# The turn from attention to feed-forward in a transformer layer on 8 cores: one of Z's buffers moved, GpSimd's and ScalarE's steps put in another order, loads issued at other places, and one tile's x1 written first in bf16

## The reference, cut to what matters

```python
x = x0 + attn(layernorm(x0))
x = x + ffn(layernorm(x))

def attn(src):                      # linear attention, post-norm block
    Q, K = elu(src @ Wq + bq) + 1, elu(src @ Wk + bk) + 1
    v = src @ Wv + bv
    KV = einsum('bshd,bshm->bhdm', K, v)               # sum over all 4096 tokens
    Z = 1 / (einsum('bshd,bhd->bsh', Q, K.sum(1)) + EPS)
    o = einsum('bshd,bhdm,bsh->bshm', Q, KV, Z)
    x = layer_norm(src + o @ Wo + bo, g1, be1)         # "x1" below
    y = gelu(x @ W1 + b1) @ W2 + b2                    # 1024 -> 4096 -> 1024
    return layer_norm(x + y, g2, be2)

def ffn(x):                         # Wf below: weight.T with disha added in
    return x @ weight.T + pooled(x) @ disha            # pooled: 16 groups of 64 channels summed
```

## Time and profile before

| | us |
|---|---|
| median of 3 runs | 1567.32 |
| lowest run | 1565.68 |
| profiled execution, its own time | 1555.34 |
| its span, by core | 1546.1 to 1553.4 |
| TensorE busy (page, core 1) | 1497.2 (96%) |
| VectorE busy | 977.3 (63%) |
| ScalarE busy | 516.4 (33%) |
| GpSimd busy | 418.4 (27%) |

### The profile page before, as it was taken

One profiled execution on the slowest core, in us unless ns is written; L12 is line 12 of the kernel. 1 busy time (PEld: TensorE's weight loads), 2 busy tenths in 40 slices (PEclk: granted clock), 3 DMA queues, 4 the chain that ended last, 5 costly groups with the idle time before them and its releaser, 6 DMA issues.

```text
span 1552.0 us, 26610 instructions; the slowest of 8 cores (1546.1 to 1553.4 us)
## 1 busy us (share of the span) xinstructions
PE 1497.2 (96%) x9240; PEld 889.7 (57%) x9240; DVE 977.3 (63%) x1082; ACT 516.4 (33%) x923; POOL 418.4 (27%) x404
## 2 busy tenths in 40 slices
PE   5999999998779999999999999999999999999997
PEld 2444444444446666666666666666666666666664
DVE  4676666658448575666767585665667585766234
ACT  2444444445413223232323323232323233232221
POOL 3323233222365222222231222222231222222111
PEclk9999999999899999999999999999999999999999
DMA  9979988877941312121221223121221213121121
GB/s 202 210 178 183 211 184 204 178 193 156 175 117 69 90 53 77 49 87 49 76 76 60 80 53 89 48 75 55 82 76 48 89 54 90 48 76 55 55 69 41
DMA packets 141024, 157.52 MB, mean 101 GB/s; under 512 B 94688, under 2 KB 102880, under 8 KB 140896
## 3 DMA queue, kind: packets, MB, share of 16 engines
q1 hardware_dynamic: 119568, 123.06, 26.8%
q0 software_dynamic: 14112, 25.70, 12.3%
q10 hardware_dynamic: 7216, 7.08, 1.4%
HBM read 117.53 MB, written 41.94 MB: 103 GB/s over the span
## 4 chain that ended last, share of the span: by engine, by line
PE 88%; DMA 5%; DVE 3%; issue 2%; POOL 2%; ACT 1%; SPq 0%; DVEq 0%; ACTq 0%; POOLq 0%
PE psH L1379 27%; PE psY L1357 26%; PE psY L611 12%; PE psS L892 7%; PE psS L710 6%; PE psS L582 6%; DMA arena<-Wv 2%; DMA arena<-WfT 2%; DMA qt_s<-arena 1%; DVE arena L820 1%; PE psH L590 1%; PE psS L797 1%; POOL arena L1217 0%; PE psY L582 0%; POOL arena L356 0%
## 5 line engine op out<-in xcount | busy, mean ns | idle before, releaser
L1379 PE MATMUL psH<-arena 128*128 128x256 bf16 x4096 | 533.1, 273 | 0.0
L1357 PE MATMUL psY<-arena 128*128 128x512 bf16 x2000 | 518.2, 381 | 8.0 <-ACT arena L1279 7.6
L1279 ACT ACTIVATE arena<-psH,arena 128x256 bf16<-128x256 f32 x512 | 242.9, 475 | 759.0 <-PE psH L1379 757.2
L1379 PEld LDWEIGHTS psH<-arena 128*128 128x128 bf16 x4096 | 402.0, 98 | 143.3 <-issue 0.3
L1357 PEld LDWEIGHTS psY<-arena 128*128 128x128 bf16 x2000 | 196.2, 98 | 137.6 <-issue 11.7
L820 DVE RECIPROCAL arena<-arena 128x512 f32<-128x512 f32 x60 | 200.8, 3346 | 72.1 <-ACT arena L810 72.1
L611 PE MATMUL psY<-arena 128*128 128x512 bf16 x944 | 213.2, 379 | 0.7 <-DVE arena L512 0.7
L611 PEld LDWEIGHTS psY<-arena 128*128 128x128 bf16 x944 | 91.0, 98 | 105.2 <-issue 1.1
L759 POOL TENSOR_TENSOR arena<-arena 128x1024 f32<-128x1024 f32 x32 | 68.8, 2154 | 230.4 <-ACT arena L755 222.3
L705 POOL TENSOR_TENSOR arena<-arena 128x1024 f32<-128x1024 f32 x32 | 68.1, 2128 | 229.8 <-ACT arena L700 229.8
L333 POOL TENSOR_TENSOR arena<-arena 128x1024 f32<-128x1024 f32 x29 | 67.7, 2333 | 201.8 <-DVE arena L518 201.3
(11 more groups left out here) (129 smaller groups left out, 1304.4 us busy)
## 6 DMA issues: line engine op xcount, KB each, us to landing
arena<-x SPq DMA_DIRECT2D x64, 512.0 KB, 4.8
xb_s<-arena SPq DMA_DIRECT2D x32, 512.0 KB, 6.0
arena<-W POOLq DMA_DIRECT2D x64, 256.0 KB, 7.9
arena<-xb_s SPq DMA_DIRECT2D x32, 512.0 KB, 3.2
out<-arena SPq DMA_DIRECT2D x31, 512.0 KB, 2.9
arena<-qt_s SPq DMA_DIRECT2D x16, 512.0 KB, 3.2
qt_s<-arena ACTq DMA_DIRECT2D x26, 256.0 KB, 8.4
arena<-WfT SPq DMA_DIRECT2D x16, 256.0 KB, 2.8
```

Source lines behind the costliest of these rows:

```text
L1279: sc.activation(h_buf(n)[:, :], hbank[n % 2], AF.Gelu, bias=b1c[:, c:c + 1]).then_inc(b_g, 1)
L1357: ii = te.matmul(ybank[k], h_buf(n)[:, (k // 2) * P:(k // 2 + 1) * P], w2_v[c][:, (k % 2) * HALF:(k % 2 + 1) * HALF], start=(c == 0), stop ...
L1379: ii = te.matmul(hbank[n % 2], w1_v[c // NCH][:, w, (c % NCH) * P:(c % NCH + 1) * P], x1T[i % 2][:, w, :], start=(w == 0), stop=(w == NCH ...
```

## The change

1. `ring(1, even)` moves to a free place, so `den_out(1, 0)` no longer waits for the q stores; `den_out(1, 1)` does.
2. GpSimd: four of the last five W2 loads are issued before W1 part 1. Part 2 is issued before the factors of pair 0 (`t_rstd(0, ..)`) instead of behind them. Part 3 waits for the q stores. The factors of pair 1 move up by two sums of Wf each.
3. SyncE: the first two pieces of Wf are loaded before the last q stores.
4. Tile 1 (`0, 1`): VectorE writes x1 straight into `nb` in bf16, and once more in float32 behind it; ScalarE's `x1_cast(0, 1)` is gone. TensorE does `q_proj(62)` before the transposes.
5. `last_prep` moves before the last tile's K addition, and `src_norm(0, ..)` before its exp. ScalarE inverts Z's last part before `q_exp(57)`, and VectorE scales with it before `m_out(15)`.
6. gelu 0 waits for all but the last q chunk, gelu 2 for all; `src_norm` moves to other steps; `b2_add` waits for the float32 x1 too.

```diff
@@ ring, pool_a, act_a, dve_a
         def ring(j, k):
             if j == 1:
-                return VF(W + 40960 + 2048 * (k % 2), HALF)
+                return VF(W + (55296, 40960)[k % 2], HALF)
...
+            w2_load(27)
+            w2_load(28)
...
+                if t == T - 1:
+                    sc.wait_ge(f_nm, 1)
+                    src_norm(sc, 0, 0)
+                    src_norm(sc, 0, 1)
                 k_exp(t)
...
-                if t == T - 1:
-                    last_prep(v)
                 k_in(t)
                 k_out(t)
                 if t < T - 1:
                     q_out(v, 2 * (t - 4))
+                if t == T - 2:
+                    last_prep(v)
@@ b2_add, den_out
             gp.wait_ge(b_x1b, 2 * j + sub + 1)
+            gp.wait_ge(b_x1, 2 * j + sub + 1)
...
-            elif j == 1:
+            elif j == 1 and k == 1:
                 sc.wait_ge(s_qst[1], 32 * NG)
@@ wf_in, sync_f
+        def wf_in(sy, h):
+            c, lo = h // 2, HALF * (h % 2)
+            sy.dma_start(zring[h % 2], wf_d[c * P:(c + 1) * P, lo:lo + HALF]
+                         ).then_inc(s_wf[h % 2], 16)
...
-            sy.wait_ge(b_src, 2)
             x_in(sy, 1, 0)
             x_in(sy, 1, 1)
             sy.dma_start(qs1[:, :, :, :], qt_d[1]).then_inc(s_q1, 16)
             q_store(sy, NG - 2, 1)
+            sy.wait_ge(f_q, 4)
+            for h in range(2):
+                wf_in(sy, h)
             q_store(sy, NG - 1, 0)
             q_store(sy, NG - 1, 1)
@@ pool_f
             bo_add(gp, 0, 1)
+            for c in (29, 30):
+                gp.dma_start(w2_v[c][:, :], w2_d[c * P:(c + 1) * P, :]).then_inc(s_w2, 16)
...
-            t_rstd(gp, 0, 0)
-            t_rstd(gp, 0, 1)
             gp.wait_ge(f_m, 16)
             for w in range(NCH):
                 gp.dma_start(w1_v[2][:, w, :],
                              w1_d[w * P:(w + 1) * P, 2 * D:3 * D]).then_inc(s_w1[2], 16)
+            t_rstd(gp, 0, 0)
+            t_rstd(gp, 0, 1)
             gp.wait_ge(a_q, NCH * NG)
+            gp.wait_ge(s_qst[1], 32 * NG)
             for w in range(NCH):
                 gp.dma_start(w1_v[3][:, w, :],
...
-            for c in range(27, NFCH):
-                gp.dma_start(w2_v[c][:, :], w2_d[c * P:(c + 1) * P, :]).then_inc(s_w2b, 16)
+            c = NFCH - 1
+            gp.dma_start(w2_v[c][:, :], w2_d[c * P:(c + 1) * P, :]).then_inc(s_w2b, 16)
@@ act_f, dve_f
             m_out(12)
+            z_inv(3)
             q_exp(sc, QL + 3)
-            z_inv(3)
...
-            x1_cast(sc, 0, 1)
...
             m_out(14)
+            z_mul(3)
             m_out(15)
             q_out(v, QL + 3)
-            z_mul(3)
...
             t_stats(v, 0, 1)
+
+            hm, n = home(0, 1), 2
+            v.wait_ge(b_mvt, n)
+            v.scalar_tensor_tensor(hm[:, :], hm[:, :], mvt[1][:, 0:1], g1b[:, :], ALU.subtract,
+                                   ALU.mult).then_inc(b_gt, 1)
             q_out(v, QL + 5)
-            x1(v, 0, 1)
-            for n in range(QL + 6, NCH * NG):
+            v.wait_ge(b_gt, n)
+            v.wait_ge(b_rt, n)
+            v.wait_ge(b_tx, 1)
+            v.scalar_tensor_tensor(nb[:, :], hm[:, :], rt[1][:, 0:1], be1b[:, :], ALU.mult,
+                                   ALU.add).then_inc(b_x1b, 1)
+            q_out(v, QL + 6)
+            v.scalar_tensor_tensor(hm[:, :], hm[:, :], rt[1][:, 0:1], be1b[:, :], ALU.mult,
+                                   ALU.add).then_inc(b_x1, 1)
+            for n in range(QL + 7, NCH * NG):
                 q_out(v, n)
@@ pe_f, sync_b
             q_proj(te, QL + 7)
+            q_proj(te, QL + 8)
             x1_tr(te, 0, 1, hbf)
-            q_proj(te, QL + 8)
             q_proj(te, QL + 9)
...
-                sy.wait_ge(f_q, 4)
-                for h in range(16):
...
+                for h in range(2, 16):
+                    sy.wait_ge(b_ws, h - 1)
+                    wf_in(sy, h)
@@ pool_b, act_b
-                for h in range(4, 10):
+                for h in range(4, 8):
                     w_sum(h)
                 t_rstd(gp, 1, 0)
-                w_sum(10)
-                w_sum(11)
+                w_sum(8)
+                w_sum(9)
                 t_rstd(gp, 1, 1)
-                for h in range(12, 16):
+                for h in range(10, 16):
                     w_sum(h)
...
                 if n == 0:
+                    sc.wait_ge(a_qt, NCH * NG - 1)
+                    sc.wait_ge(s_rows, 48)
+                elif n == 2:
                     sc.wait_ge(a_qt, NCH * NG)
-                    sc.wait_ge(s_rows, 48)
...
-                if c in (5, 7) and not post:
-                    src_norm(sc, 1, (c - 5) // 2)
+                if c in (2, 5) and not post:
+                    src_norm(sc, 1, c // 4)
...
-                if c == 28 and far:
+                if c == (28 if post else 30) and far:
                     src_norm(sc, i + 2, 0)
@@ y_step
             if n == 0:
-                te.wait_ge(s_w2, 16 * 27)
+                te.wait_ge(s_w2, 16 * (NFCH - 1))
...
-            if n == 27:
-                te.wait_ge(s_w2b, 16 * (NFCH - 27))
+            if n == NFCH - 1:
+                te.wait_ge(s_w2b, 16)
```

More of the change, by code:

```diff
@@ L986, in z_inv @@
                 sc.activation(zring[k % 2], zring[k % 2], AF.Exp, scale=-1.0).then_inc(f_z, 1)
-            sc.wait_ge(f_nm, 1)
-            src_norm(sc, 0, 0)
-            src_norm(sc, 0, 1)
             q_exp(sc, QL)
@@ L1175, in sync_b @@
                 sy.dma_start(dsh2[:, :], dsh_d).then_inc(s_dsh, 16)
-                sy.wait_ge(f_q, 4)
-                for h in range(16):
-                    c, lo = h // 2, HALF * (h % 2)
-                    if h >= 2:
-                        sy.wait_ge(b_ws, h - 1)
-                    sy.dma_start(zring[h % 2], wf_d[c * P:(c + 1) * P, lo:lo + HALF]
-                                 ).then_inc(s_wf[h % 2], 16)
+                for h in range(2, 16):
+                    sy.wait_ge(b_ws, h - 1)
+                    wf_in(sy, h)
                 sy.wait_ge(b_ws, 16)
```

## The result

The changed kernel took 1555.22 us in the median (1551.18 to 1557.54, five runs), the kernel before 1566.95 (1564.39 to 1721.02, five runs): ratio 0.9927, 95% interval 0.9903 to 0.9952. That is 11.7 us gained where 22.3 were forecast, and the time is 0.2 us outside the range. The profiled execution took 1551.18 us.

What follows compares the result with a forecast made beforehand. TensorE's 27 us of idle time and 7.1 us of clock between 345 and 490 us gave a 34 us ceiling; shifts summed to 16.1 at `attn(1, 0)`, then 21.2, then 22; 1567.3 - 22.3 = 1545 us, range 1538 to 1555.

Steps and rivals of the forecast that it cites:

- What costs nothing: Side effects held free: early W2 loads, and eight part 2 issues (4.6 us) before tile 0's factor, with 3 us of cover.
- The second rival: GpSimd is held issuing part 2 until part 1 lands; tile 0's factor 8 us late, gain 17 to 18, 1549 us; 17%.
- End of the passes: Last tile's K addition: with `last_prep` a tile earlier, TensorE's wait at the column sums goes; 1.1 us.
- Z's last part: Block 0: ScalarE no longer does `q_exp(57)` before inverting Z's last part, so TensorE gets the result 1.1 us earlier.
- Tile 1: Transposes of tile 1: `q_proj(62)` fills the wait and the cast leaves the chain; 2.9 of 3.6 us won.
- gelu: Gelu's table load no longer waits for the last `q_out`: 0.9 of 2.7 us won, bounds 0 and all of it.
- Z of pair 1: `den_out(1, 0)` no longer waits for the q stores: 4.9 us won; 1.1 us more from VectorE's wait before `attn(1, 0)`.
- T: The landing of the last q stores, taken as 403.5 us, with bounds 398.1 (quiet) and 409.7 (as slow as before).
- as slow as before: Upper bound of the q stores' landing: T = 409.7; everything behind D moves by 6 us, gain 16, 1551 us; 12%.
- The transpose at the twentieth step: Pair 1's factor runs before two sums of Wf, saving 5 us; 3.1 of TensorE's 8.1 us wait stay.
- D: Landing of the last casting load, from which GpSimd's fourth sum of Wf starts: 440.5 us before, forecast 424.4.
- Clock: TensorE's mean clock of 0.94 costs 7.1 us; 4.1 come back by `attn(1, 0)`, about 1 us more later.

Runs made afterwards that it cites:

- the factors first: Changed kernel with GpSimd's factors of pair 0 ahead of the eight loads of W1 part 2 again: 1539.39 us, ratio 0.9792.
- the split version: Changed kernel with five loads of W1 part 2 ahead of pair 0's factors, three behind: 1537.60 us, ratio 0.9777; run again 1537.79 us, ratio 0.9743.
- the two versions with more semaphores: Changed kernel, no instruction moved, W1 part 1's loads on eight semaphores instead of one: 1536.35 us, ratio 0.9829; on two: 1537.69 us, one execution.
- the half ring: Changed kernel with GpSimd's descriptor ring halved (`dynamic_dma_scratch_size` 1024 for 2048): 1567.17 us, one execution.

## Why the prediction was wrong

**The step that failed** is the one in "What costs nothing": "Eight issues of 0.57 us now precede the factor of tile 0 ... done by 376 ... That is 3 us of cover." 0.57 us is right for each issue (0.53 measured), but the eight are not one stretch: the fifteenth unfinished load is the sixth of part 2, and it waits until part 1 has landed. On core 0 the factor ran 36.5 us after the first product of the column sums, where the step had it due at 379.3 - 355.3 = 24.0; without the hold it ran at 23.8 to 26.3. Price: 8 to 9 us to the end.

**The second rival is what happened**, with 17%, and it was mis-sized three ways. It named part 2's fourth load as the fifteenth, by counting the two early W2 loads; both had landed (5.3 to 6.0 us after issue) and the hold came two loads later. It let part 1 land at 384.5, 29.2 us after the column sums' first product; it was 33.1 to 34.6. Part 1 was issued 0.8 us later than that working has it, and its slowest load took 23.6 to 25.0 us, for 20.4 in the earlier trace rows (20.3 to 21.8 over the cores). The two W2 loads are not shown to be the reason, since part 1's first load took as long as before (9.7 to 11.2 us for 9.9 to 11.2), nor is part 2, since with the factors first it was issued after part 1 had landed and the slowest load still took 23.2 to 24.6. Two pieces of Wf are now loaded in that time; that was not tested. And it let the loss shrink to 4 or 5 us at the twentieth step, since the sums of Wf were to be late anyway; but with the hold TensorE's own way is the later one there, no wait is left at those transposes on any core, and the whole 8 to 9 stay.

**Without the hold the sum was right, in part by luck.** In the split version attention (2, 0) starts 112.1 us after the first product of the column sums, 21.1 earlier than before in the median of the cores. The forecast of 22.3 was made on core 1, whose own mark before is 134.4, so it says 112.1 as well. On the way there it was off: attention (1, 0) was to start at 418.5 - 355.3 = 63.2 and started at 66.6, and the transposes of (1, 0) at 85.5 and started at 86.8. Most of the 3.4 us of delay went into the wait that the forecast had left at those transposes, and the rest was made good behind them: from there to attention (2, 0) it is 25.3 us for 28.0 before. By terms:
- *End of the passes, 1.1, and Z's last part, 1.1*: no wait at L1124's successor, and the transposes of tile 0 at 29.5 to 29.6 on the three cores without a wait for the first q load, for 31.9: both terms are there. On the other cores that wait, of up to 2.3 us, takes them away again (30.8 in the median). "What costs nothing" had put it at nothing; before there was none.
- *Tile 1, 2.9, and gelu, 0.9*: taken back, 3.7 and 0.7 us.
- *Z of pair 1, 4.9 and 1.1*: taken back, 3.2 to 4.1. T was forecast 48.2 us after the first product; the last store landed at 50.5 to 53.6, nearer to the bound "as slow as before" (54.4), so ScalarE still waits up to 4.5 us for `den_out(1, 1)` and TensorE up to 2.5. The term is 2 too large; the rest of the 3.4 us lies in the clock's share and in the wait for the q load, which no run separates.
- *The transpose at the twentieth step, 5.0 and a wait of 3.1 left*: taken back, 5.2 to 6.6; 0.6 to 0.8 of wait left in the median, up to 3.3. D as the start of the sums was not borne out: the fourth sum started at 68.3 to 74.4 (the forecast has 69.4), and on every core 3.0 to 4.5 us before the last casting load had landed.
- *Clock*: 0.94 became 0.96 in the changed kernel and 0.99 in the split version (core 4):

```profile
345.00:490.00 145.00, 134.04 (x852) 80.15 (x867) 104.89 (x112) 61.50 (x105) 69.78 (x71) 0.99 0.65 147
```

Of the 21 us some 18 to 19 reach the mean span. The 21.1 us are whole at every attention of the later blocks (the last starts 1077.8 us after the first product before, 1056.7 in the split version), so the rest is lost at the end: from TensorE's last product to the end of the span it is 4.3 to 5.4 us on the eight cores of the split version, and 3.4 to 3.6 on seven of before's. Why stays open.

**The rule of the Trainium skill** on GpSimd's descriptors beside a busy VectorE ("SBUF — State Buffer", section "SBUF: two separate sides") was rightly left out of the sum: the issues took 0.53 to 0.63 us with VectorE busy, before and after, and the long idle time follows the landings in every version. These runs do not test the rule itself: it is about operations that take both ports, and beside part 1 VectorE mostly ran casts out of PSUM (0.7 us each). Its 1557 us, 2 from the result, would have been right by accident. The Trainium skill's rule that queues are served packet by packet ("DMA: Bandwidth & Descriptors", section "Queues, rings and completion order") doesn't make a store quick here: under load they took 9.6 to 14.1 us on core 4 in the split version run again, and 11.0 in the median before.

**The base was off as well**, in the other direction. The gain was taken from the median of 1567.3, while the profiled execution had 1555.34. On the later chips most executions of before carried a pair of cores at 0.97, and the changed kernel 1 of 5, so its median of 1546.63 there lies inside the forecast's range with the hold still in it: the number agrees, the mechanism does not. On the first chip the changed kernel in turn lost some 7 us ahead of the change: in the passes of cores 0 to 3 the clock was 0.94 to 1.00 in stretches of 50 us, where the kernel before has 1.00 from 50 us on, and the column sums began at 360.4 to 363.0 in place of 353.9 to 355.3: the mean span of cores 0 to 3 was 1549.1 there, of cores 4 to 7 1540.5, as on the second chip. Both moved the ratio. That loss in the passes is not the hold's; whether the rarer slow pairs come from the change is open.

## What to carry to other kernels

An engine that issues loads can be stopped by the queue's room, and everything behind it on that engine stops too: here after 14 unfinished loads. Count the loads that are under way, not the time of their issues, and read every "issue" gap of the profile of before against the landings until one rule explains all of them; here the start of this program, where single landings let single loads go, and the pause in part 3, where all eight had to land, together suggest the rule that the two versions with more semaphores bear out. A step on which others wait goes ahead of the loads that may be held, or the loads get semaphores of their own, which here gave the same mean span as the split (1531.1 for 1531.6) and moves nothing.

## What the runs showed of the hardware

- GpSimd's queue takes 14 unfinished loads of 128 rows (7 with half the scratch), then holds the engine. It goes on 0.3 to 0.4 us after the oldest load is known to be done; of loads that count on one semaphore that is when all have landed (397.5 and 397.88 in the changed kernel), with two semaphores the first four, with eight each by itself. That the count is what the engine looks at is the reading of these times, not something a row names.
- A pair of cores can fall behind together. In the profiled execution of the changed kernel on the second chip cores 6 and 7 were granted 0.81, between the two levels (1.2 and 2.4 GHz), for some 160 us from shortly after the stall at tile 0, though TensorE was busy again all the while; cores 0 to 5 had a stall of 6.4 to 9.2 us there, cores 6 and 7 of 8.3 and 5.2, and the six came back to 1.00. Timeline by stretch of core 7 (columns: us, busy, count, clock, DMA, GB/s):

```profile
400.00:420.00 20.00, 18.00 (x102) 0.77 0.86 163
460.00:500.00 40.00, 40.00 (x230) 0.81 0.16 53
530.00:560.00 30.00, 30.00 (x167) 0.81 0.30 88
560.00:600.00 40.00, 40.00 (x259) 0.99 0.18 51
```

It costs those cores 20 us. Some pair had a mean clock of 0.97 in 20 of 28 executions of before, in 1 of 5 of the changed kernel on the second chip, in 1 of 3 with pair 1's factors back (which brings a stall of 5 us at the twentieth step), and in 1 of 24 of the versions that have all other terms and no hold; the half ring, with the longest stall, did not show it in its one execution, so the length of the stall alone does not set it. Why stays open.
